# AdaLN convolution and LoRA feed-forward on one core: the prologue's loads, context, and first merges in another order

## What is computed

```python
N = 64 sequences, 64 channels, L = 1024          # x: (64, 64, 1024), float32
y = conv1d(x, weight, padding=4, groups=4)       # 9 taps, 16 channels in and out of each group
y = y + (cond @ c_weight.T)[:, :, None] + cond_bias[None, :, None]
base  = y @ kernel + bias                        # 1024 x 1024
A_eff = einsum('bn,nri->bri', gate, lora_A)      # 8 blocks, 16 LoRAs of rank 32
B_eff = einsum('bn,nor->bor', gate, lora_B)
delta = (y @ A_eff.T) @ B_eff.T + (y @ lora_A_shared.T) @ lora_B_shared.T
out   = x + base + delta
```

## Time and profile before

| | us |
|---|---|
| median of 3 runs | 530.34 |
| the profiled execution | 530.98 |
| its span | 529.2 |
| PE busy in the span | 510.4 |
| DVE busy | 242.3 |
| POOL busy | 207.5 |
| ACT busy | 144.8 |

### The profile page before, as it was taken

One profiled execution on the slowest core, in us unless ns is written; L12 is line 12 of the kernel. 1 busy time (PEld: TensorE's weight loads), 2 busy tenths in 40 slices (PEclk: granted clock), 3 DMA queues, 4 the chain that ended last, 5 costly groups with the idle time before them and its releaser, 6 DMA issues.

```text
span 529.2 us, 6509 instructions
## 1 busy us (share of the span) xinstructions
PE 510.4 (96%) x2372; PEld 414.0 (78%) x2372; DVE 242.3 (46%) x302; ACT 144.8 (27%) x175; POOL 207.5 (39%) x124
## 2 busy tenths in 40 slices
PE   4699989999999999999999999999999999999996
PEld 3456778888888888888888888888888888888884
DVE  3878684446243552437243462328334363424311
ACT  2545514322313141221323133220324123131000
POOL 1576954542516053341615243261605334171100
PEclk9899999999999999999999999999999999999999
DMA  8995769441834256240934247240833313141212
GB/s 216 302 242 183 159 228 220 177 112 36 199 96 112 66 141 170 76 113 11 207 106 112 75 109 179 72 116 30 202 115 90 98 53 102 24 120 48 86 41 72
DMA packets 19575, 65.05 MB, mean 123 GB/s; under 512 B 3274, under 2 KB 3914, under 8 KB 18922
## 3 DMA queue, kind: packets, MB, share of 16 engines
q1 hardware_dynamic: 17690, 63.46, 45.0%
q10 hardware_dynamic: 1872, 1.41, 1.1%
HBM read 45.59 MB, written 18.87 MB: 122 GB/s over the span
## 4 chain that ended last, share of the span: by engine, by line
PE 90%; DMA 4%; DVE 2%; POOL 1%; issue 1%; ACTq 0%; ACT 0%; DVEq 0%
PE main L793 65%; PE conv L748 16%; PE rank L806 6%; PE main L798 3%; DMA lb<-in_L_ffn_lora_B 3%; DMA x_in<-in_x 1%; DVE x_tr L537 1%; PE conv L785 1%; POOL as_st L321 1%; ACT x_hi L413 0%; PE spare L761 0%; DVE w_raw L584 0%; POOL x_lo L313 0%; DVE res L665 0%; DVE y_lo L572 0%
## 5 line engine op out<-in xcount | busy, mean ns | idle before, releaser
L335 POOL TENSOR_TENSOR y_lo<-y_stage,y_hi 128x512 fp32r<-128x512 f32 x60 | 77.6, 1295 | 242.1 <-ACT y_hi L428 242.1
L793 PE MATMUL main<-w_hi,y_hi 128*128 128x512 f32 x512 | 160.1, 391 | 1.4 <-DVE res L665 1.4
L793 PE MATMUL main<-w_lo,y_hi 128*128 128x512 f32 x512 | 159.5, 390 | 0.0
L793 PE MATMUL main<-w_hi,y_lo 128*128 128x512 f32 x512 | 159.4, 390 | 0.0
L793 PEld LDWEIGHTS main<-w_hi,y_hi 128*128 128x128 f32 x512 | 96.0, 188 | 22.4 <-issue 1.8
L793 PEld LDWEIGHTS main<-w_lo,y_hi 128*128 128x128 f32 x512 | 96.1, 188 | 20.9
L793 PEld LDWEIGHTS main<-w_hi,y_lo 128*128 128x128 f32 x512 | 96.1, 188 | 20.6
L428 ACT ACTIVATE y_hi<-y_stage 128x512 fp32r<-128x512 f32 x64 | 40.5, 632 | 236.5 <-DVE y_stage L566 236.5
L556 DVE TENSOR_TENSOR y_add<-conv,ctx_all 128x512 f32<-128x512 f32 x64 | 44.2, 690 | 121.3 <-PE conv L748 120.8
L329 POOL TENSOR_TENSOR x_lo<-x_tr,x_hi 128x1032 fp32r<-128x1032 f32 x30 | 87.9, 2929 | 25.0 <-ACT x_hi L433 25.0
L566 DVE STREAM_TRANSPOSE y_stage<-y_add 128x512 f32<-128x512 f32 x64 | 75.6, 1181 | 6.6
(11 more groups left out here) (76 smaller groups left out, 286.9 us busy)
## 6 DMA issues: line engine op xcount, KB each, us to landing
res<-in_x SPq DMA_DIRECT2D x32, 512.0 KB
out<-res SPq DMA_DIRECT2D x31, 512.0 KB
x_in<-in_x SPq DMA_DIRECT2D x28, 512.0 KB, 11.1
w_raw<-in_L_ffn_kernel SPq DMA_DIRECT2D x16, 256.0 KB, 19.0
b_cur<-b_scratch SPq DMA_DIRECT2D x21, 128.0 KB, 2.4
...
```

What stands on the lines that cost most here:

```text
L335: nc.gpsimd.tensor_tensor(y_part(y_lo, h, t, mh), y_stage[:, i % 2, :], y_part(y_hi, h, t, mh).bitcast(F32), ALU.subtract).then_inc(ylo_do ...
L793: mm(main[t][:, n * 512:(n + 1) * 512], lhs, rhs[:, k, n * 512:(n + 1) * 512], start=k == 0 and first, stop=False)
```

## The change

Seven edits, all in the prologue but for the two noted above.

1. The taps arrive as whole rows of 576 bytes in `w_nat`; DVE copies them into `w_pad`. PE transposes them before the context's operands, and ACT splits `t_hi` first.
2. ACT instead of DVE repeats `cond_w` (`cw_rep`).
3. The context's bias comes as a column per group, `cbias` [128, 4], by four small DMAs, and is added by DVE when it fills `ctx_all`; the four products with the ones and POOL's two instructions go.
4. Queues: SP starts with three of the four pieces of the first half of x, ACT has the fourth; the shared LoRA factors are all on SP; `la` goes ahead of all of W; the second half of x is issued by ACT, after `bias_hi`.
5. PE's order: mix_a 0 and 1 ahead of merge 0 and 1, mix_a 2 and 3 ahead of merge 2 and 3. Chunk 0 is cut so that the two products with `w_hi` run first, and that with `w_lo` afterwards. Chunks 1, 2 and 3 each move ahead by one place against the convolutions and mix_b.
6. DVE's order follows that, and the second four `x_turn`s stand together behind w_add 3. The four mix_b and b_turn are spread between the merges.
7. `x_in` has rows of 1056 instead of 1032 elements, with x from element 16; `convolve` takes its three products in the order hi-hi, lo-hi, hi-lo.

So w_add 4 and 5 stand right behind a block that waits for the second half of x. The diff, without the declarations of semaphores and tiles that only change name:

```diff
+
+EDGE = 16
+ROW = EDGE + L + EDGE
...
-        x_in = sb("x_in", [P, CL, L + 2 * HALO])
+        x_in = sb("x_in", [P, CL, ROW])
...
+            ("w_pad", [C, CG, PAD + TAPS + PAD], F32), ("w_nat", [C, CG * TAPS], F32), ("cond_nat", [NS, CD], F32), ("cw_nat", [C, CD], F32),
+            ("cond_t", [CD, NS], F32), ("cw_rep", [P, G, J, CG], F32), ("cbias", [P, G], F32),
...
-                eng.dma_start(x_in[ch * 32:(ch + 1) * 32, :, HALO + at:HALO + end],
+                eng.dma_start(x_in[ch * 32:(ch + 1) * 32, :, EDGE + at:EDGE + end],
...
         @block.sync
         def _(sp):
-            sp.dma_start(cbias[:, :], cond_bias.rearrange("(a c) -> a c", a=1)).then_inc(cbias_in, 16)
+            load_first(sp, 0, (0, 1, 2))
             sp.dma_start(gate_nat[:, :], gate).then_inc(gate_in, 16)
-            load_first(sp, 0, (0, 1))
-            load_shared(sp, 0)
-            load_shared(sp, 1)
-            load_first(sp, 1, (0, 1))
+            with nc.allow_non_contiguous_dma(reason="small"):
+                for g in range(G):
+                    sp.dma_start(cbias[:, g:g + 1], bass.AP(cond_bias.tensor, cond_bias.offset + g * CG, [[0, J], [1, CG], [1, 1]])
+                                 ).then_inc(cbias_in, 16)
+            for q in range(3):
+                load_shared(sp, q)
             for oh in range(2):
                 sp.dma_start(bias_nat[oh * 8:(oh + 1) * 8, :], bias_v[oh]).then_inc(bias_in, 16)
-            load_w(sp, 0)
             for q in range(RQ):
                 sp.dma_start(la[:, q, :], la_v[:, q, :]).then_inc(la_in[q], 16)
-            for ma in range(1, 4):
+            for ma in range(4):
                 load_w(sp, ma)
...
-            nc.gpsimd.memset(ones[:, :], 1.0).then_inc(biasrep_done, 1)
-            pool.wait_ge(cbias_in, 16)
-            nc.gpsimd.tensor_copy(bias_rep[:, :, :, :], cbias[:, :].rearrange("a (g c) -> a g c", g=G)
-                                  .unsqueeze(2).broadcast_to([1, G, J, CG])).then_inc(biasrep_done, 1)
...
-            act.dma_start(w_pad[:, :, PAD:PAD + TAPS], conv_w).then_inc(cw_in, 16)
+            act.dma_start(w_nat[:, :], conv_w.rearrange("o c k -> o (c k)")).then_inc(cw_in, 16)
             act.dma_start(cond_nat[:, :], cond).then_inc(cond_in, 16)
             act.dma_start(cw_nat[:, :], cond_w).then_inc(cond_in, 16)
-            load_first(act, 0, (2, 3))
-            load_shared(act, 2)
-            load_first(act, 1, (2, 3))
-            act.wait_ge(cond_tr, 1)
-            nc.scalar.activation(cond_t[:, :], rank[:, 0:NS], ACT.Copy).then_inc(cond_cp, 1)
+            load_first(act, 0, (3,))
...
+            act.wait_ge(cond_tr, 1)
+            nc.scalar.activation(cond_t[:, :], rank[:, 0:NS], ACT.Copy).then_inc(cond_cp, 1)
+            nc.scalar.activation(cw_rep[:, :, :, :], rank[:, NS:NS + C].rearrange("p (g c) -> p g c", g=G)
+                                 .unsqueeze(2).broadcast_to([P, G, J, CG]), ACT.Copy).then_inc(cwrep_done, 1)
...
             nc.scalar.activation(bs_st[0:STACK, :], bs_t[0:STACK, :], ACT.Copy).then_inc(bs_hi, 1)
             act.wait_ge(bias_in, 32)
             nc.scalar.activation(bias_hi[:, :], bias_nat[:, :], ACT.Copy).then_inc(bias_split, 1)
+            load_first(act, 1, range(CH))
...
-            dve.wait_ge(pad_zero, 2)
             dve.wait_ge(cw_in, 16)
+            nc.vector.tensor_copy(w_pad[:, :, PAD:PAD + TAPS], w_nat[:, :].rearrange("o (c k) -> o c k", k=TAPS)).then_inc(pad_done, 1)
+            dve.wait_ge(pad_done, 3)
             wide = PAD + TAPS + PAD
             nc.vector.tensor_copy(z_all[:, :, :, :], bass.AP(w_pad[:, :, :].tensor, 0, [[CG * wide, C], [1, WIN], [wide, CG], [1, J]])
                                   ).then_inc(z_done, 1)
...
-                blocks = x_in[:, :, :].rearrange("p c (m j) -> p m c j", j=J)[:, m0:m1]
+                blocks = x_in[:, :, EDGE - HALO:EDGE + L + HALO].rearrange("p c (m j) -> p m c j", j=J)[:, m0:m1]
...
-            nc.vector.tensor_copy(ctx_all[:, :, :], rank[:, 256:512].rearrange("p (g n) -> p g n", g=G)).then_inc(ctx_done, 1)
+            dve.wait_ge(cbias_in, G * 16)
+            nc.vector.tensor_tensor(ctx_all[:, :, :], rank[:, 256:512].rearrange("p (g n) -> p g n", g=G),
+                                    cbias[:, :].unsqueeze(2).broadcast_to([P, G, NS]), ALU.add).then_inc(ctx_done, 1)
...
             dve.wait_ge(ctx_done, 1)
             y_tile(0, 0, 0, FIRST, first=True)
             y_tile(0, 0, 1, FIRST, first=True)
+            a_turn(0)
+            a_turn(1)
+            y_first_low(0)
+            y_first_low(1)
             w_add(0)
             w_add(1)
-            y_first_low(0)
-            y_first_low(1)
-            dve.wait_ge(x_first[1], 64)
-            x_turn(0, 4)
-            a_turn(0)
-            x_turn(0, 5)
-            a_turn(1)
+            a_turn(2)
+            a_turn(3)
             w_add(2)
             w_add(3)
-            x_turn(0, 6)
-            x_turn(0, 7)
-            a_turn(2)
-            a_turn(3)
+            dve.wait_ge(x_first[1], 64)
+            for c in range(XH, XC):
+                x_turn(0, c)
             x_first_low(1)
...
             y_first_low(3)
             b_turn(0)
-            b_turn(1)
             w_add(10)
             w_add(11)
+            b_turn(1)
+            w_add(12)
+            w_add(13)
             b_turn(2)
             b_turn(3)
-            nc.vector.memset(x_in[:, :, 0:HALO], 0.0).then_inc(halo_zero, 1)
-            nc.vector.memset(x_in[:, :, HALO + L:], 0.0).then_inc(halo_zero, 1)
-            for m in range(12, 16):
+            nc.vector.memset(x_in[:, :, EDGE - HALO:EDGE], 0.0).then_inc(halo_zero, 1)
+            nc.vector.memset(x_in[:, :, EDGE + L:EDGE + L + HALO], 0.0).then_inc(halo_zero, 1)
+            for m in range(14, 16):
                 w_add(m)
...
-            pe.wait_ge(cond_in, 32)
-            nc.tensor.transpose(rank[:, 0:NS], cond_nat[:, :], ident[0:NS, 0:NS])
-            nc.tensor.transpose(rank[:, NS:NS + C], cw_nat[:, :], ident[0:C, 0:C]).then_inc(cond_tr, 1)
...
                 last.then_inc(t_tr, 1)
+            pe.wait_ge(cond_in, 32)
+            nc.tensor.transpose(rank[:, 0:NS], cond_nat[:, :], ident[0:NS, 0:NS])
+            nc.tensor.transpose(rank[:, NS:NS + C], cw_nat[:, :], ident[0:C, 0:C]).then_inc(cond_tr, 1)
             pe.wait_ge(cond_cp, 1)
             pe.wait_ge(cwrep_done, 1)
-            pe.wait_ge(biasrep_done, 2)
             for g in range(G):
                 cols = rank[:, 256 + g * NS:256 + (g + 1) * NS]
-                mm(cols, cw_rep[:, g, :, :].rearrange("p j c -> p (j c)"), cond_t[:, :], start=True, stop=False)
-                last = mm(cols, bias_rep[:, g, :, :].rearrange("a j c -> a (j c)"), ones[:, :], start=False, stop=True)
+                last = mm(cols, cw_rep[:, g, :, :].rearrange("p j c -> p (j c)"), cond_t[:, :], start=True, stop=True)
             last.then_inc(ctx_mm, 1)
...
-                for lhs, rhs in ((t_hi, x_hi), (t_hi, x_lo), (t_lo, x_hi)):
+                for lhs, rhs in ((t_hi, x_hi), (t_lo, x_hi), (t_hi, x_lo)):
...
-            def dense(h, t, k, halves=(0, 1)):
+            def dense(h, t, k, halves=(0, 1), products=(0, 1, 2)):
                 yh, yl = y_hi[h][:, t, k, :], y_lo[h][:, t, k, :]
-                for lhs, rhs, first in ((yh, w_hi, True), (yh, w_lo, False), (yl, w_hi, False)):
+                for i in products:
+                    lhs, rhs, first = ((yh, w_hi, True), (yh, w_lo, False), (yl, w_hi, False))[i]
                     for n in halves:
                         mm(main[t][:, n * 512:(n + 1) * 512], lhs, rhs[:, k, n * 512:(n + 1) * 512],
                            start=k == 0 and first, stop=False)
...
             convolve(0, 0, 0, FIRST, first=True)
             convolve(0, 0, 1, FIRST, first=True)
+            mix_a(0)
+            mix_a(1)
             merge(0)
             merge(1)
-            mix_a(0)
-            mix_a(1)
+            mix_a(2)
+            mix_a(3)
             merge(2)
             merge(3)
-            mix_a(2)
-            mix_a(3)
-            merge(4)
-            merge(5)
...
-            chunk(0, (0,))
+
+            pe.wait_ge(y0_lo, 2)
+            pe.wait_ge(whi_done, 1)
+            dense(0, 0, 0, products=(0, 2))
             pe.wait_ge(a_done, RQ)
-            chunk(0, (1,))
+            dense(0, 1, 0, products=(0, 2))
+            pe.wait_ge(wlo_done, 1)
+            for t in range(2):
+                dense(0, t, 0, products=(1,))
+            merge(4)
+            merge(5)
+            chunk(1)
             convolve(0, 0, 2, FIRST, first=True)
             merge(6)
             merge(7)
-            chunk(1)
+            chunk(2)
             convolve(0, 0, 3, FIRST, first=True)
             merge(8)
             merge(9)
-            chunk(2)
+            chunk(3)
             mix_b(0)
-            mix_b(1)
             merge(10)
             merge(11)
-            chunk(3)
-            mix_b(2)
```

(4 more changed lines are left out.)

23 lines of the change are left out of this document (9 added, 14 removed).

## The result

The changed kernel takes 545.9 us (median of 4 runs, 544.86 to 547.54), the kernel before 530.4 beside it: ratio 1.030, 95% interval 1.026 to 1.033. It is 15.5 us slower. The prediction was 529.4, in a range that ended at 532.5. The profiled execution took 546.06 with a span of 544.3, against 530.98 and 529.2. One run of those reported further down, of e11_old_tail, took 1312.88 us where its other three took 536.27 to 541.61, and is left out of its median.

A forecast was written before the change was run, and what follows sets the result against it. PE bounds the kernel from 66 us on, unchanged, so only the prologue can gain: a 4.2 us earlier start shrinks to 1.2 behind `lb`, 0.9 after a possible DVE delay, giving 529.4 us; 8-in-10 range 527.7 to 532.5.

The forecast's parts named there:

- The first convolution starts at 11.1: Start of the prologue: PE's first convolution begins at 11.1 instead of 15.30, 4.2 us earlier.
- They cost between 0 and the 1.9 us: Start: the bias's four small DMAs ahead of the factors on SP cost 0 to 1.9 us, covered because POOL is last.
- w_add 2 and 3 [end at] 26.4: Middle of the prologue: w_add 2 and 3 end at 26.4, so chunk 1 can start at 30.0, PE idle 2.1 us.
- I take 28.5: Landing of x's second half: 28.5, between 27.6 at 94 GB/s and 29.2 at 82; chunk 2 then starts at 38.2.
- it flows from 17: Load of x's second half: ACT issues it at about 15.7 and it flows from 17.
- its last 0.5 MB ran in 13.7 to 19.0: ACT's queue in the kernel before: its last 0.5 MB ran then, at most 94 GB/s, a rate used for x.
- rival A: x's second half late: landing at 29.2 or 32.2 gives 530.1 or 533.1, about 531.6 in the middle; chance 0.20.
- The sentence on the Trainium skill: Queues alternate by packet: x's short rows get a third or less, 77 GB/s, landing at 30.0, program 530.9.
- Chunk 3 is ahead of mix_b 0 now: End of the prologue: 2.74 us less work behind mix_b 0; `convolve(0, 1, 0)` 1.2 us earlier, the rest becoming two waits.
- I leave its landing at 46.35: Load of factor B (`lb`): same bytes ahead, so it still lands at 46.35, with 1 us to either side.
- Rival B: Clock drops to the 1.2 GHz level after PE's 3.6 us gap before chunk 2: 531.1; chance 0.12.
- rivals C and D: C: all 4.2 us of the start carry through, 526.1, chance 0.08. D: `lb` and x early, 528.3 at best, 0.15.

The follow-up runs named there:

- e11_old_tail: Changed kernel with loads issued nearly as in the kernel before, and the old order of work behind merge 3: 537.7 us.
- e5: Changed kernel with x's second half on SP's queue behind W 0, between W 0 and W 1: 535.9 us.
- e16: Changed kernel with x's second half on SP's queue behind W 0 and cbias's four transfers left out, tile set to zero: 531.8 us.
- e4: Changed kernel, x's second half still late on ACT's queue, with W's transfers in rows of 2048 instead of 8192 bytes: 536.4 us.
- e2: Kernel before, with only x's second half taken from its early places and issued late by ACT behind bias_hi: 543.8 us.
- e10: Kernel before, with only the changed kernel's order of PE and DVE work behind mix_a 3: 535.0 us.
- e18: Changed kernel with x's second half behind W 0 on SP, cbias as one 256-byte transfer, and the old order behind merge 3: 533.5 us.

## Why the prediction was wrong, point by point

- "The first convolution starts at 11.1": 12.11. Right in kind. The taps' whole rows landed at 4.5 and not at 2.9, later than in the kernel before (3.92), and the added copy took 0.23 (0.25 taken).
- "They cost between 0 and the 1.9 us": cbias's transfers left a hole in the traffic (142 GB/s in 8 to 10 us), and by e5 and e16 cost the program some 3 to 5 us. The bound was taken from another transfer's delay. The cover named, POOL being last, was wrong: the shared factors behind them came late, DVE waited 2.17 us for `bs_rep` and POOL stood 1.71 us ahead of `as_st`, so merge 0 began at 22.03 and not at 19.6. W's and `la`'s bytes behind them had no cover either.
- "w_add 2 and 3 [end at] 26.4": w_add 0 started at 29.25. The step counted mix_a and a_turn and forgot that W 0 itself was now queued behind 2 MB of `la`. PE waited 3.45 us.
- "I take 28.5": the step that failed. x's second half had landed at 45.2. Two things were wrong in it. "it flows from 17": nothing of it flowed before 24. And the rate: 50 to 55 GB/s while it flowed, below the slower bound of 66. The rates came from stretches in which ACT's queue ran against rows of 2000 to 4096 bytes; the new place put it beside 8192-byte rows for its whole length. One of them was misread besides: "its last 0.5 MB ran in 13.7 to 19.0" does not hold, for the DMA view of the kernel before has for ACT's queue in that stretch

```profile
q10 hardware_dynamic: 25, 0.03, 2.7%
```

  so the 94 GB/s are nobody's rate. This is rival A with the right mechanism, "each us of it goes straight to the end", and 16.7 us of lateness instead of up to 4; e5 and e4 measure it at 9.5 to 10 us of time, e2 at 12.8 in the kernel before.
- The sentence on the Trainium skill took "4,096 and more" for the neighbour's rows and got a third. With W's 8192 it gives 20% of 220 GB/s, 43, and from the forecast's start at 17 a landing at 41. The measured share was 24%; the rest of the 45.2 is the late start.
- "Chunk 3 is ahead of mix_b 0 now": the new tail was booked as a gain that turns into two waits. e10 shows that it costs 4.6 us in the old kernel: the wait for w_lo was worked out once, for chunk 1, and not carried on to chunks 2 and 3.
- "I leave its landing at 46.35": only e18 comes near (47.7). In e5 mix_b 0 waited for `lb` until 54.0. The bytes ahead were the same, but 4.99 MB instead of 6.30 had flowed by 24 us. 0.59 MB of the difference lie in 10 to 14, where the old order had both queues at work, at 347 GB/s against 201; the rest is not settled.
- Rival B came as a companion, twice: the granted clock was 0.50, the 1.2 GHz level, in 32 to 36 us, behind the 3.45 us wait, and again in 46 to 58, with 1.85 us more for chunk 2 alone. The first had the 8.11 us wait for x behind it, which covers it.
- Right: nothing after the prologue changed its pace; rivals C and D were rightly small.

Along one line of runs the 15.5 us add up: 545.9, 535.9 with x's second half behind W 0 (e5), 531.8 with cbias's transfers left out (e16), 530.4 before. That is 10.0 for x, 4.1 for cbias and 1.4 for all the rest, or 10.1, 2.8 and 2.8 by the ratios. The tail's 4.6 us of e10 do not fit in beside them: there it was measured in the old kernel, where nothing had been won ahead of it, while e16 starts its first convolution 2.6 us earlier and still waits for w_lo (1.61, 0.94 and 2.00 us). e18, with all three undone but `la` still ahead of W, is 3 above before. So each cost depends on the state of the others, and `lb`'s arrival caps what a faster front can win.
